# Half-row gate loads, attention products moved between slots, and unread products on TensorE, in a transformer block on one core

## What is computed

```python
def reference(x, f, cond, ...):             # x, f: 4 x 256 x 256
    h = bi_wkv(x, f, f, w, u, cond)         # forward and backward decayed scans over the tokens
    qkv = h @ Wqkv.T + bqkv                 # 16 heads of 16 channels
    attn = softmax((q @ k.T) * 4.0)
    x = x + (attn @ v) @ Wproj.T + bproj
    h = bi_wkv(x, f, f, w2, u2, cond)
    scores = sigmoid(h @ gate_w.T)          # 64 experts: best 4 of 8 groups, then best 6
    w_dense = ...                           # 1024 x 64 weights, zero where not chosen
    routed = (relu2(h @ w1.T) * w_dense) @ w2.T
    shared = relu2(h @ shared_up.T) @ shared_down.T
    return x + routed + shared
```

## Time and profile before

| | |
|---|---|
| median of 3 runs | 625.95 us (624.86 to 629.41) |
| profiled execution | 627.93 us, of which 626.1 us is the span from first to last instruction |
| mean granted TensorE clock | 0.793 of full speed |
| TensorE busy | 400.3 us, 64% of the span |
| VectorE busy | 310.4 us, 50% |
| ScalarE busy | 203.9 us, 33% |
| GpSimd busy | 129.6 us, 21% |
| DMA | 50.9 MB, the 16 DMA engines 33.1% busy on average |

### The profile page before, as it was taken

One profiled execution on the slowest core, in us unless ns is written; L12 is line 12 of the kernel. 1 busy time (PEld: TensorE's weight loads), 2 busy tenths in 40 slices (PEclk: granted clock), 3 DMA queues, 4 the chain that ended last, 5 costly groups with the idle time before them and its releaser, 6 DMA issues.

```text
span 626.1 us, 5613 instructions
## 1 busy us (share of the span) xinstructions
PE 400.3 (64%) x1580; PEld 287.2 (46%) x1580; DVE 310.4 (50%) x552; ACT 203.9 (33%) x392; POOL 129.6 (21%) x117
## 2 busy tenths in 40 slices
PE   0526877688725646768985866672756566576664
PEld 0315554555514435546764654451444444454442
DVE  7779566663462332445653538532433434344343
ACT  3224325533503222244652523321232322323232
POOL 5164315120101010123221221210211212112121
PEclk9957567969657777778998976778878878778889
DMA  7792355142670121212322222222222222232221
GB/s 190 105 169 35 35 67 69 22 49 32 130 111 17 60 93 64 75 56 76 105 79 92 78 94 79 93 71 71 93 90 81 78 93 93 78 92 78 92 97 70
DMA packets 33952, 50.91 MB, mean 81 GB/s; under 512 B 3146, under 2 KB 15626, under 8 KB 33930
## 3 DMA queue, kind: packets, MB, share of 16 engines
q1 hardware_dynamic: 33930, 50.65, 33.1%
HBM read 39.16 MB, written 1.33 MB: 65 GB/s over the span
## 4 chain that ended last, share of the span: by engine, by line
DMA 30%; SPq 28%; PE 18%; DVE 11%; issue 7%; ACT 3%; POOL 1%; DVEq 0%; ACTq 0%; POOLq 0%
SPq L305 20%; DMA ex<-gates 17%; SPq L309 5%; DMA q_st<-nmax_lo 5%; DMA clip<-in_tiles 4%; DMA k_st<-qk_lo 3%; PE ps L1188 3%; PE ps L1243 3%; SPq L343 2%; DVE mx L867 2%; DVE scan L814 2%; DVE t_lo L1019 2%; DVE scan L1098 2%; SPq L351 2%; PE ps L1211 2%
## 5 line engine op out<-in xcount | busy, mean ns | idle before, releaser
L483 POOL TENSOR_TENSOR scan<-scan 128x512 f32<-128x512 f32 x68 | 72.8, 1071 | 372.9 <-ACT scan L647 361.0
L1321 PE MATMUL ps<-hid_hi,t_hi 128*128 128x512 f32 x136 | 71.0, 522 | 91.2 <-DVE t_lo L1019 91.2
L1103 DVE TENSOR_TENSOR qk_lo<-scan,qk_hi 128x512 fp32r<-128x512 f32 x68 | 70.4, 1036 | 70.3 <-ACT qk_hi L657 69.4
L1019 DVE TENSOR_TENSOR t_lo<-clip,t_hi 128x512 fp32r<-128x512 f32 x68 | 47.5, 699 | 102.8 <-ACT t_hi L637 102.7
L637 ACT ACTIVATE t_hi<-clip 128x512 fp32r<-128x512 f32 x68 | 42.6, 627 | 155.3 <-DMA clip<-in_tiles 140.4
L1321 PEld LDWEIGHTS ps<-hid_hi,t_hi 128*128 128x128 f32 x136 | 31.0, 228 | 117.6 <-DVE t_lo L1019 59.1
L1098 DVE TENSOR_TENSOR scan<-scan,ex 128x512 f32<-128x512 f32 x68 | 49.5, 728 | 64.6 <-DMA ex<-gates 42.9
L1211 PE MATMUL ps<-k_st,q_st 96*128 96x256 f32 x128 | 37.2, 384 | 61.5 <-DVE mx L867 53.8
L1332 PE MATMUL ps<-qk_hi,t_hi 128*128 128x512 f32 x136 | 64.3, 473 | 7.4 <-DVE qk_lo L1103 7.3
L1323 PE MATMUL ps<-hid_hi,t_lo 128*128 128x512 f32 x136 | 65.4, 481 | 0.0
L1322 PE MATMUL ps<-hid_lo,t_hi 128*128 128x512 f32 x136 | 64.7, 476 | 0.0
(11 more groups left out here) (123 smaller groups left out, 495.1 us busy)
## 6 DMA issues: line engine op xcount, KB each, us to landing
clip<-in_tiles SPq DMA_DIRECT2D x68, 256.0 KB, 14.6
ex<-gates SPq DMA_DIRECT2D x68, 256.0 KB
q_st<-qk_hi SPq DMA_DIRECT2D x16, 128.0 KB, 3.9
q_st<-qk_lo SPq DMA_DIRECT2D x16, 128.0 KB, 4.9
k_st<-qk_hi SPq DMA_DIRECT2D x16, 128.0 KB, 5.9
k_st<-qk_lo SPq DMA_DIRECT2D x16, 128.0 KB, 6.6
f_sb<-in_fT SPq DMA_DIRECT2D x4, 256.0 KB, 8.6
x_sb<-in_xT SPq DMA_DIRECT2D x4, 256.0 KB, 9.4
```

The source lines that it names most:

```text
L483: g.tensor_tensor(sq[:, k], relu[:, k], relu[:, k], ALU.mult).then_inc(sq_ready, 1)
L1103: TT(act_lo[:, k], act[:, k], act_hi[:, k].bitcast(F32), ALU.subtract).then_inc(act_lo_ready, 1)
L1321: mm(bank_h(bank), w_hi, x_hi, start=(c == 0), stop=False)
```

## The change

There are four parts.

1. `load_spread` issues two DMAs of 64 partitions, one for each expert row, in place of one with a 2 x 64 source.
2. From batch 1 on, q and k go through DRAM: `store_qk` writes the high and low parts (four DMAs a batch, rows of 1 KB), and `load_stack` reads them back with six DMAs a half batch, rows of 8 KB.
3. Work moves between slots. A projection is split over two slots, k's and v's come later, `hidden1` and the scans come a slot or two earlier, the tails, the first two gate products and both routers come later, and `GAP` goes from 1 to 2. The bias of v is no longer added by products with one row (line 1191, two for each batch; a float32 product stands in the trace as two instructions). It goes once, multiplied with the output weights, into the bias of the residual (`project_bias`).
4. `keep_busy` puts two products of 512 columns into bank 4, which nobody reads, ahead of the shifted scores of a head. That is done for 23 heads of periods 0 to 2, in 22 slots.

```diff
-GAP = 1
+GAP = 2
@@ jobs, and slots of the tails
+            return [n // 4 for n in range(3, H * B, 4) if head_slot(n) + (2 if n in (H + 7,) or n == 7 else 1) == g]
-            return head_slot(H * b + H - 1) + 2
+            return head_slot(H * b + H - 1) + (4, 3, 2, 2)[b]
@@ sync
-                sp.dma_start(spread[:, k], gates[t, :, half * HT:(half + 1) * HT].unsqueeze(1).broadcast_to([2, P // 2, HT])
-                             ).then_inc(ld_spread[k], 16)
+                for r in range(2):
+                    sp.dma_start(spread[r * (P // 2):(r + 1) * (P // 2), k],
+                                 gates[t, r, half * HT:(half + 1) * HT].unsqueeze(0).broadcast_to([P // 2, HT])
+                                 ).then_inc(ld_spread[k], 16)
...
+            def store_qk(b):
+
+                for w in range(2):
+                    for n, (part, ready) in enumerate(((qk_hi, qk_hi_ready), (qk_lo, qk_lo_ready))):
+                        sp.wait_ge(ready, 4 * b + 2 * w + 2)
+                        sp.dma_start(qk_dram[w, b, :, n].rearrange("t d (h s) -> (d h) t s", s=S),
+                                     part[:, w].bitcast(F32)).then_inc(st_qk[w], 16)
...
+                    if b > 0:
+                        sp.wait_ge(st_qk[w], 32 * b)
+                        src = qk_dram[w, b, half]
+                        width = STACK // (2, 4)[w]
+                        for r in range(0, STACK, width):
+                            rows = src.rearrange("n d s -> (n d) s") if w == 0 else src[r // (STACK // 2)]
+                            sp.dma_start((q_st, k_st)[w][r:r + width, n].rearrange("p h s -> p (h s)").bitcast(F32),
+                                         rows).then_inc(ld_stack[n], 16)
+                        continue
...
             for b in range(B - 1):
+                store_qk(b + 1)
                 load_rows(b, 0)
                 load_stack(b + 1, 0)
@@ tensor
-                    if name == "v":
-                        last = mm(job_bank(job)[:, t * S:(t + 1) * S], k_st[MAXROW:MAXROW + 1, 0, 0, 0:P].bitcast(F32),
-                                  bvb[MAXROW:MAXROW + 1, :], start=False, stop=True, skip_group_check=True)
...
+            def keep_busy(n, groups):
+
+                b, half, h = n // H, n % H // HB, min(n % HB, HB - 2)
+                pe.wait_ge(bias_sum, 1)
+                if groups > 0:
+                    pe.wait_ge(o_raw_ready, groups)
+                for kt in range(QT):
+                    mm(ps[:, 4, :], k_st[0:MAXROW + 2, slot(b, half), h, kt * P:(kt + 1) * P],
+                       q_st[0:MAXROW + 2, slot(b, half), h:h + 2, :], start=True, stop=True)
...
                 for n in shifted_at(g):
+                    if n % HB and not values_at(g - 1):
+                        keep_busy(n, groups)
                     shifted_scores(n // H, n % H)
...
-                if s == 2:
-                    project(b + 1, "q")
+                if s in (1, 2):
+                    project(b + 1, "q", s - 1)
...
-                if s == 4:
-                    project(b + 1, "k")
+                if s - (4, 4, 5)[b] in (0, 1):
+                    project(b + 1, "k", s - (4, 4, 5)[b])
...
-                if s == (10, 10, 6)[b]:
-                    project(b + 1, "v")
+                if s - (11, 11, 12)[b] in (0, 1):
+                    project(b + 1, "v", s - (11, 11, 12)[b])
```

More of the change, by code:

```diff
@@ L81, in bass_adaln_attn_ffn @@
         gw = sb("gw", [P, KC, E])
-        bvb = sb("bvb", [P, C])
+        bias = sb("bias", [P, KC])
+        bvs = sb("bvs", [P, KC])
         gbb = sb("gbb", [P, E])
@@ L170, in bass_adaln_attn_ffn @@
         fill_ready, ld_fill = sem("fill_ready"), sem("ld_fill")
+        st_qk = [sem(f"st_qk{w}") for w in range(2)]
         ld_stack = [sem(f"ld_stack{n}") for n in range(SLOTS)]
@@ L219, in bass_adaln_attn_ffn @@
         jobs = [("q", 0), ("k", 0), ("v", 0)]
[L220 to L226, removed]
+        jobs += [("q", 1), ("k", 1), ("m", 0, 0), ("v", 1), ("m", 0, 1)]
+        jobs += [("q", 2), ("k", 2), ("m", 1, 0), ("v", 2), ("ot", 0, 0), ("ot", 0, 1), ("m", 1, 1), ("oc", 0)]
+        jobs += [("proj", 0), ("q", 3), ("k", 3), ("m", 2, 0), ("ot", 1, 0), ("ot", 1, 1), ("gate", 0), ("oc", 1),
+                 ("proj", 1), ("v", 3), ("m", 2, 1)]
+        jobs += [("gate", 1), ("wt", 0), ("m", 3, 0), ("ot", 2, 0), ("ot", 2, 1), ("oc", 2), ("proj", 2), ("m", 3, 1), ("gate", 2)]
         jobs += [("ot", 3, 0), ("ot", 3, 1), ("oc", 3), ("proj", 3), ("gate", 3), ("wt", 1)]
@@ L258, in unit_bank, with stacked @@
             return n % 2 if n >= ALONE else 1
+        def stacked(b, half):
+            return 96 * turn(b, half) + (32 if slot(b, half) < 2 else 0)
         def unit_at(s):
@@ L388, in _ @@
                 next_spread(n, 0, n, n % RING)
-            for s in range(HB - 1, HEAD + 1):
-                if s + 1 >= 2 * RING and s + 1 < HEAD:
-                    n = s + 1
+            for s in range(HB - 1, HEAD + 2):
+                n = s + RING + 2 - ENTRY - GAP
+                if 2 * RING <= n < HEAD:
                     next_raw(n, n % NT, n % RING)
-                n = s - 1
+                n = s + RING - ENTRY - GAP
                 if n == NT + SHARED:
@@ L652, in round_act @@
                 if isinstance(n, int) and n == 0:
-                    for half in range(KC):
-                        sc.wait_ge(ld_stack[slot(B - 1, half)], 128 * turn(B - 1, half))
+                    for w in range(2):
+                        sc.wait_ge(st_qk[w], 32 * (B - 1))
                 if not isinstance(n, int) or n >= 2:
@@ L1044, in _ @@
             num_den(1, 0, 1)
+            dve.wait_ge(bias_ready, 1)
+            TT(bias[:], ps[:, 4, S:S + KC], vec[:, V_BP:V_BP + KC], ALU.add).then_inc(bias_sum, 1)
             for g in range(H * (B - 1)):
@@ L1295, in turn_weights @@
                 last.then_inc(job_sem(job), 1)
-            pe.wait_ge(ld_w, 32)
+            pe.wait_ge(ld_w, 16)
             for name in "qk":
-                project(0, name)
+                for t in range(KC):
+                    project(0, name, t)
             pe.wait_ge(ident_ready, 1)
@@ L1303, in _, with project_bias @@
             pe.wait_ge(ld_fill, 48)
-            project(0, "v")
+            for t in range(KC):
+                project(0, "v", t)
+            def project_bias():
+                pe.wait_ge(ld_wo, 32)
+                for t in range(KC):
+                    for c in range(KC):
+                        last = mm(ps[:, 4, S + t:S + t + 1], wo[:, c, t * P:(t + 1) * P], bvs[:, c:c + 1],
+                                  start=(c == 0 and t == 0), stop=(c == KC - 1), skip_group_check=True)
+                last.then_inc(bias_ready, 1)
+            project_bias()
             def up(n, half, k, s):
@@ L1368, in _ @@
                         project_out(c)
-                    if t == 8 and c == 1:
-                        gate(c)
-                if s == 15:
-                    turn_max(b, 1)
             for s in range(HEAD + ENTRY + GAP):
@@ L1379, in _ @@
                     scores(B - 1, s + 1)
-                if s == 4:
+                if s == 0:
+                    gate(1)
+                if s == 5:
                     turn_weights(0)
```

87 lines of the change are left out of this document (49 added, 38 removed).

## The result

The changed kernel takes 440.69 us (median of 4 runs, 439.3 to 445.58) where the kernel before, on the same chip, took 625.4: a ratio of 0.706 [0.699, 0.713], or 29% less. The prediction was 446 us. The profiled execution took 441.25 us, 439.5 of it span.

A forecast was written before the change was run, and what follows sets the result against it. Two DMA engines were taken to bound the units. Span 42 + 107 + 88 + 194 + 12 = 443 us, with 1.8 around it 445, stated as 446 us; range 422 to 472 (8 in 10: 422 to 510).

The forecast's parts named there:

- Two DMA engines bound the units: In the units, gates use about 2 of 16 DMA engines and tiles queue behind them, 6.07 us a unit.
- The first rival: In the units, gate halves use only some engines: up to 4.5 us a unit, 537 us at most; chance 0.11.
- The turns of the hardware loop: Units: seven loop turns, hidden so far behind the wait for tiles, cost 4 us in all.
- Short products, batch 3's VectorE steps and its waits: Units: some 90 short products cost 9 us, batch 3's other VectorE steps 3, its tail's cross-engine waits 5.
- The second router: Units: the router's VectorE work over four slots, 18.8 against 12.2 us, costs 7 us.
- The start: Units: the first of these units starts 4 us after the last score.
- what the clogged engines did to others: Period 3: late rows of maxima and late first gates, 12 + 7 + 4.5 us, of which 22 us go.
- one unit less: Period 3: one unit less stands there through GAP, worth 7.4 less some 3 us, so 4 us off.
- The stacks: Periods 0 to 2: six long-row loads land about 4 us earlier, 8 us off; stores cost 1 us a period.
- The moves and the bias rows: Periods 0 to 2: bias rows 5 us off, v projection about 3, moves 3 (between 10 off and 3 on).
- The unread products: Periods 0 to 2: 46 products cost TensorE 11 to 20 us, a higher clock saves 14; net -1 us taken.
- The mark that the clock would rise above 0.8: Periods 0 to 2: sign of the forecast, TensorE's clock rising from 0.72 to above 0.8.

The follow-up runs named there:

- split_only: The kernel before with only the gates' load split into two DMAs of 64 rows: 463.61 us, ratio 0.737 to the kernel before.
- undo_split: The changed kernel with the gates loaded again as one DMA with a 2 x 64 source: 591.1 us, ratio 0.937 to the kernel before.
- sbuf_stacks: The changed kernel with each later stack loaded again from SBUF in eight loads, without the way through DRAM: 458.94 us.
- after_again: The changed kernel itself, unaltered, run again beside other runs on the same chip: 442.08 us.
- router_slow: The changed kernel with four second-router steps a slot in place of six, and its weights turned one slot later: 443.12 us.
- no_unread: The changed kernel without the 46 unread products: 444.22 us.
- double_unread: The changed kernel with each pair of unread products issued twice, 92 products in all: 448.71 us.

## Why the prediction was right

446 us was forecast and 440.7 measured, and the mechanism that carries the forecast, the gates on two DMA engines, is the one that it named. In the smaller terms part of the agreement is luck: errors of 3 to 8 us stood against each other, as the points below show. The stages of the changed kernel against the terms (us):

| stage | before | predicted | measured |
|---|---|---|---|
| start, to the first maximum | 42 | 42 | 42.5 |
| periods 0 to 2 | 123.5 | 107 | 104.2 |
| period 3 | 114.5 | 88 | 93.7 |
| units | 334 | 194 | 187.0 |
| tail | 12.1 | 12.1 | 12.1 |

**Two DMA engines bound the units.** Right. All five marks that the prediction set for the units came in: the DMA share is never below 0.21 in a slice of 1 us, a tile takes 0.37 us to issue, squares follow at 2.80 us, TensorE is busy all the time at clock 1.00, and ScalarE waits for TensorE. The runs with 2 and 4 as the outermost dimension settle why. The first rival (halves on some engines only) had feared that a source step of zero limits a load to five engines; each half of the gates has that step outermost, and its unit of 4.5 us didn't come. (Its 1.6 x 57 is 91 and not 93 us, as its 537 has it.)

**The terms of the units.** Ten steps at 3.04 and 47 at 2.80 us are 162, and the steps came as forecast: where nothing else stands between them, squares beside shifted scores follow at 3.04 or 3.05 us and those of units alone at 2.80. The rest is 25 us, where 32 was forecast. By the starts of the squares and rectifies it divides so:

- The turns of the hardware loop, put at 4 us, can't be seen: units follow at 2.71 to 2.89 us through all of them, 2.80 on average.
- Short products, batch 3's VectorE steps and its waits, put at 9 + 3 + 5 = 17 us, cost some 10: the sixteen units before the router's steps (squares at 248.56 to 305.29 us) take 56.7 us where the steps alone are 47.
- The second router, put at 7 us, cost 10: from the rectify at 304.55 us to that at 331.30 it is 26.75 us for six units of 2.80.
- The start, put at 4 us, has the 5 that are left.

VectorE's timeline in the router (start, length), then TensorE's (with its idle time before, and who ended it):

```profile
308.35 1.75 DVE L968 RECIPROCAL score<-gex 128x256 f32<-128x256 f32 x1
...
312.51 0.68 DVE L1135 TENSOR_TENSOR qk_lo<-scan,qk_hi 128x512 fp32r<-128x512 f32 x1
...
318.32 1.48 DVE L1011 TENSOR_TENSOR scan<-scan,gpen 128x64 f32<-128x64 f32 x4
...
321.52 1.25 DVE L1027 SCALAR_TENSOR_TENSOR num<-scan,score 128x256 f32<-128x256 f32 x1
322.69 0.68 DVE L1135 TENSOR_TENSOR qk_lo<-scan,qk_hi 128x512 fp32r<-128x512 f32 x1
```

```profile
313.25 0.51 PE L1376 MATMUL ps<-qk_hi,t_hi 128*128 128x512 f32 x1 [3.13 <-DVE qk_lo L1135]
...
323.43 0.50 PE L1376 MATMUL ps<-qk_hi,t_hi 128*128 128x512 f32 x1 [2.75 <-DVE qk_lo L1135]
```

I had shared the router's VectorE time evenly over four slots. It lies in lumps of 4.5 us in two of them, so TensorE stands for 3.13 and 2.75 us, and after each stop its next nine products take 3.7 us, mostly 0.43 us each in place of 0.234, some 1.6 us more each time. The two stops and the slow products after them are 9 of the 10 us.

**Period 3.** The chain of a slot, kept by the forecast, is there (6 to 7 us). The term for what the clogged engines did to others was 22 us, plus 4 for one unit less. The split alone gives 16.8 of the 22 in the kernel before (`split_only`) and 11.8 in the changed kernel (`undo_split`); from `split_only` to the changed kernel another 4.0 go (97.7 to 93.7), which is what one unit less was put at, though other moves lie in that step too. I had counted nearly all of the long issues of the earlier trace rows as won. That the router and the gates' own path lay beside them is my reading, not a run's. The mark for it held: all eight rows of the maxima's low parts land within 2.3 us. Not seen by the forecast: the maximum stood behind 1.3 us of work that nobody waited for, and moving it was worth 16.7 us, more than the 12.5 of the stacks.

**Periods 0 to 2.** The total was off by 3 us, the shares by more. The stacks were put at 8 less 3 for the stores, so 5, with the reason that six loads land earlier. They gave 12.5 (116.3 of `sbuf_stacks` against 103.8 of `after_again`), for the other reason above: ScalarE's wait for the buffers, which stands in the waits of before and which I had not read. The moves and the bias rows, put at 11 with the v projection, are what remains between `split_only` (123.0) and `sbuf_stacks` (116.3), once the 2.6 us that the unread products add are put back: 9.3, if the parts simply add. No run has the moves or the bias rows by themselves, so how they share it stays open. The unread products were put at -1 net; they are +2.6. The mark that the clock would rise above 0.8 came true (0.83), and for the wrong reason: without the products it is 0.83 too, and with the stacks through SBUF it is 0.78 in spite of them. It is 0.72 in `split_only`, 0.78 with part 2 undone and 0.83 with nothing undone, so it rose as waits of TensorE went; that the waits are the reason is argued and not shown.

## What to carry to other kernels

A DMA whose outermost dimension was 2 ran on two engines here, and one of 4 on four. Look for it where the DMA share of a short stretch is low (0.13 is 2 of 16, 0.25 is 4) while a queue issues without a pause or an engine waits for the transfers, and write the transfer with a large outermost dimension (64 here), even as several transfers. When an engine waits for a transfer, it may be for the transfer's source buffer: read who writes that buffer next before crediting a faster load. On an engine that serves two chains, put first the step that another engine waits for, and price filler products for the clock by running the kernel without them: here 46 of them cost 2.6 us and gave nothing.

## What was not expected of the hardware

- The last eight slots of period 3, with the same instructions and 183 products on TensorE, took 54.8 to 55.4 us at a clock of 0.92 in three kernels (the changed one, `after_again`, `router_slow`) and 60.2 to 60.7 us at 0.78 to 0.80 in three others (`no_unread`, `double_unread`, `sbuf_stacks`). Executions of the changed kernel itself lie between 439.3 and 446.06 us, the longer ones at a lower mean clock (0.873 against 0.896). What decides it wasn't found. So a difference of under 5 us between two of these kernels is read by stages only.
- The same VectorE step (L1135, 128x512) takes mostly 1.1 to 1.2 us when it starts while GpSimd squares and 0.68 us when GpSimd stands. It then ends 0.5 to 0.6 us after the square does (a square from 343.25 to 344.29 us, the step from 343.66 to 344.84), as if it began only behind it. In the steady units it is the long one 28 times of 29, and that is what brings VectorE so near to being the bound.
